# Differential attention with a post-norm feed-forward layer on one core: the attention's loops over the heads written out on every engine

## The reference, cut to what matters

```
q1, q2, k1, k2, v = x @ Wq1, x @ Wq2, x @ Wk1, x @ Wk2, x @ Wv        # split into 16 heads
a1 = softmax(causal(q1 @ k1.T / 4));  a2 = softmax(causal(q2 @ k2.T / 4))
out = (a1 - lam[h] * a2) @ v                                           # lam from lq1, lk1, lq2, lk2
merged = normalise_over_32(out) * (1 - LAM_INIT), heads side by side
x = layernorm(x + merged @ Wo)
h = silu(x @ w1.T * s1) * (x @ w2.T * s2);  h = gelu(h @ h1.T * hs1);  h = gelu(h @ h2.T * hs2)
x = layernorm(x + h @ w3.T * s3)
```

## Time and profile before

| | |
|---|---|
| three runs | 2097.49, 2097.8, 2099.39 us; median 2097.8 us |
| span of the profiled execution | 2091.4 us, 6.4 us under the median of the runs; its own time is not listed apart |
| mean granted TensorE clock | 0.961 of full speed |
| PE, ACT, DVE, POOL busy | 1925.5, 1468.2, 724.6, 201.2 us |
| first and last exponential (L811) | 232.88 us, 1311.27 us (end of the last group) |
| ACT idle just before an exponential | 106.6 us in 56 places, all ended by PE's scores (L830) |

### The profile page before, as it was taken

How to read it: one execution, slowest core, us unless ns; L and a number is a source line. 1 busy time by engine, 2 the same in 40 slices (tenths; PEclk the granted TensorE clock), 3 DMA queues, 4 the chain that set the end, 5 groups by cost and what they waited for, 6 DMA issues and landing times. The chain is left out here.

```text
span 2091.4 us, 36204 instructions
## 1 busy us (share of the span) xinstructions
PE 1925.5 (92%) x12400; PEld 1090.7 (52%) x12400; DVE 724.6 (35%) x1543; ACT 1468.2 (70%) x1876; POOL 201.2 (10%) x300
## 2 busy tenths in 40 slices
PE   7994599999899899998999999399999999999997
PEld 5883233333233233332333333278888888888886
DVE  5775021222122221221122212344554535445442
ACT  5663499989899899898998999254444435445452
POOL 0001111111111111111111111000000000000000
PEclk9997699999999999999999999699999999999998
DMA  8997805643366235642564340200101000110000
GB/s 264 361 354 200 134 6 78 83 62 55 51 82 83 36 51 81 83 56 32 79 82 57 52 57 11 81 1 31 31 11 31 22 22 21 33 31 11 11 11 12
DMA packets 137064, 148.83 MB, mean 71 GB/s; under 512 B 76000, under 2 KB 108256, under 8 KB 133760
## 3 DMA queue, kind: packets, MB, share of 16 engines
q1 hardware_dynamic: 134768, 140.55, 33.8%
q10 hardware_dynamic: 1888, 5.24, 1.3%
q0 software_dynamic: 240, 0.66, 0.2%
HBM read 90.85 MB, written 55.57 MB: 70 GB/s over the span
## 5 line engine op out<-in xcount | busy, mean ns | idle before, releaser
L811 ACT ACTIVATE attn_probs<-attn_s_ps 128x1024 f32<-128x1024 f32 (+2 forms) x1152 | 1013.5, 1049 | 112.8 <-PE attn_s_ps L830 106.6
L850 PE MATMUL attn_sums_ps<-attn_probs,heads_v 128*32 128x512 f32 (+3 forms) x5120 | 611.9, 551 | 0.0
L830 PE MATMUL attn_s_ps<-heads_q,heads_k 50*128 50x512 f32 (+3 forms) x2560 | 475.0, 435 | 93.4 <-DMA heads_q<-shift 48.5
L830 PEld LDWEIGHTS attn_s_ps<-heads_q,heads_k 50*128 50x128 f32 x2560 | 218.1, 188 | 577.3 <-ACT attn_probs L811 465.8
L1334 ACT ACTIVATE split_whole<-split_hid_ps,hs 128x512 f32<-128x512 f32 x128 | 88.3, 690 | 274.5 <-PE split_hid_ps L1248 274.3
L895 DVE COPY attn_sums_sb<-attn_sums_ps 128x512 f32<-128x512 f32 x64 | 44.3, 692 | 670.4 <-PE attn_sums_ps L850 666.8
L795 POOL TENSOR_SCALAR_AFFINE_SELECT attn_probs<-attn_probs 128x512 f32<-128x512 f32 x256 | 161.2, 639 | 955.8 <-ACT attn_probs L811 954.6
L1248 PE MATMUL split_hid_ps<-split_hid_b,h2t_r 128*128 128x512 f32 x1024 | 240.6, 392 | 0.0
L1248 PE MATMUL split_hid_ps<-split_hid_a,h1t_r 128*128 128x512 f32 x1024 | 238.1, 391 | 0.0
L1248 PEld LDWEIGHTS split_hid_ps<-split_hid_a,h1t_r 128*128 128x128 f32 x1024 | 190.0, 188 | 41.2 <-DVE split_hid_a L1476 1.4
L1248 PEld LDWEIGHTS split_hid_ps<-split_hid_b,h2t_r 128*128 128x128 f32 x1024 | 189.8, 188 | 38.0
(11 more groups left out here) (123 smaller groups left out, 1567.2 us busy)
## 6 DMA issues: line engine op xcount, KB each, us to landing
qk_parts<-proj_parts SPq DMA_DIRECT2D x64, 512.0 KB, 5.6
heads_q<-qk_parts SPq DMA_DIRECT2D x90, 256.0 KB
heads_k<-qk_parts SPq DMA_DIRECT2D x90, 256.0 KB
proj_w_rows<-in_L_ffn_h_w SPq DMA_DIRECT2D x16, 512.0 KB, 6.5
values<-proj_v SPq DMA_DIRECT2D x8, 1024.0 KB, 6.0
diffs<-attn_diff SPq DMA_DIRECT2D x32, 256.0 KB, 4.5
split_heads<-diffs SPq DMA_DIRECT2D x8, 1024.0 KB, 5.5
heads_v<-values SPq DMA_DIRECT2D x15, 512.0 KB
```

Source lines behind the costliest of these rows:

```text
L811: nc.scalar.activation(weights, side_by_side, ACT.Exp, scale=SCALE).then_inc(exp_done, 1)
L830: last = nc.tensor.matmul(s_ps[n % SLOTS][:, s, place * width:(place + 1) * width], k_sb[u][rows, b * SEQ + j * PARTS:b * SEQ + (j + 1) * ...
L850: last = nc.tensor.matmul(sums[c * D:(c + 1) * D, off:TILE], v_sb[u][:, b * KEY_BLOCKS + j, :], probs[k % PROBS][:, b, s, off:TILE], start ...
```

## The change

Every loop over the heads in the attention becomes a Python loop, which writes the code of all 16 heads one behind the other, on PE, SP, ACT, POOL and DVE. The head number is then a constant: no jump and no register operation is left there, and all waits compare with constants. The computation, the buffers, the semaphores and the order of the engines' work instructions stay as they are. Line numbers behind L763 fall by three.

```diff
-        def all_heads(eng, head):
-
-            head(0, 0, 0, True, False)
-            with eng.Fori(0, (HEADS - 2) // 2) as i:
-                head(2 * i + 1, 1, i, False, False)
-                head(2 * i + 2, 0, i + 1, False, False)
-            head(LAST, LAST % 2, LAST // 2, False, True)
+        def all_heads(head):
+
+            for h in range(HEADS):
+                head(h, h % 2, h // 2, h == 0, h == LAST)
...
-            all_heads(sp, head)
+            all_heads(head)
...
-            with pool.Fori(0, HEADS) as h:
+            for h in range(HEADS):
...
-            with act.Fori(0, HEADS) as h:
+            for h in range(HEADS):
...
-            all_heads(pe, head)
+            all_heads(head)
...
-            with dve.Fori(0, HEADS) as h:
+            for h in range(HEADS):
```

## The result

| | before | after |
|---|---|---|
| median | 2097.64 us (2093.87 to 2099.39, 4 runs) | 2058.75 us (2057.12 to 2059.86, 4 runs) |
| ratio, 95% interval | | 0.9819 [0.9805, 0.9833] |
| span of the profiled execution | 2091.4 us | 2057.0 us |
| first exponential to end of the last | 232.88 to 1311.05, 1078.2 us | 232.95 to 1273.18, 1040.2 us |
| end of the last exponential to end of the span | 780.35 us | 783.8 us |

The change is worth 38.9 us by the medians. The forecast was 2052.0, its range 2044 to 2063: the direction and the range held, the single value is 6.8 us too low. 34.4 us of the gain are in the two profiled spans: 37.9 in the attention, less 3.5 that the finish gives back.

What follows compares the result with a forecast made beforehand. ACT and PE were taken as balanced bounds at 64.34 us a head, with six heads lengthened by PE's taken jumps. Those jumps gave 45.8 us, all other terms 0: 2097.8 - 45.8 = 2052.0 us, range 2044 to 2063.

Steps and rivals of the forecast that it cites:

- Item 1: Attention: removing PE's six taken jumps gains 45.8 us, 7.6 each, by whole windows; silence alone would give 33 us.
- Item 2: Attention: removing PE's register operations is worth nothing, within 0.1 us a head.
- Item 3: Attention: removing jumps and register operations of ACT, POOL and DVE gains 0, at most 16.8 us in 16 heads.
- Item 4: Attention: loading written-out code, new for four engines, costs 0, at most 47 us for ACT's 14 packets.
- 250 instructions: Code loading: the estimate of how many PE instructions one 16 KB packet on q8 holds.
- Item 5: Attention: PE's code pages under the head loads cost 0, with up to 10 us kept in the range.
- rival B: Attention: PE's pages come late in 5 to 8 heads, giving 10 to 25 us back, 2062 to 2077; 8%.
- Item 6: Finish: PE's loop keeps two taken jumps, its place in a code page shifts; 0, bounds -3 to +7 us.
- The base: Whole kernel: the median of the runs is 6.4 us over the span, and the change leaves that alone.
- Rival A: Attention: register waits cost too, so ACT's gaps of 0.37 and 0.17 us go, 8.6 us more, 2043; 5%.

Runs made afterwards that it cites:

- e2: Changed kernel with only PE's and SP's head loops written out; ACT, POOL and DVE keep theirs with register waits: 2051.91 us, ratio 0.9789.
- e12: Kernel before with only PE's head loop written out; SP, ACT, POOL and DVE keep theirs: 2052.29 us, ratio 0.9798.
- e5: Changed kernel, but on PE and SP heads 1 to 12 stand in a loop of two rounds, one taken jump: 2060.67 us, ratio 0.9805.
- e4: Changed kernel, but PE and SP have each pair of heads in a single-round loop, registers back, no jump taken: 2056.41 us, ratio 0.982.
- e1: Changed kernel with ACT's two waits exchanged, scores first and free buffer second: 2054.89 us, ratio 0.9805.
- e3: Changed kernel with only ACT's, POOL's and DVE's loops written out; PE and SP keep theirs: 2093.64 us, ratio 1.0002 to the kernel before.
- after_again: The changed kernel run once more without any edit: 2056.87 us, ratio 0.9813.
- e6: Changed kernel with 11 unused semaphore increments on PE at the start of each head from 2 on: 2053.37 us, ratio 0.9783.
- e8: Changed kernel with SP issuing the next head's 13 loads in groups of three, waiting for each group to land: 2056.02 us, ratio 0.979.
- e9: Changed kernel with ACT's two waits exchanged and SP's head loads in groups of three: 2051.35 us, ratio 0.9777.
- e7: Changed kernel with 11 unused PE semaphore increments a head from 2 on, and 179 more before head 0: 2083.17 us, ratio 0.9916.
- e11: Changed kernel with only PE's and SP's head loops written out, SP's loads in threes, PE's finish loop also written out: 2047.54 us, ratio 0.9767.

## Why the prediction was right, and where it was off

**Item 1, PE's jumps.** Right in mechanism and in size. In e2 and e12 fifteen heads take 15 x 64.34 = 965.1 us, where before they took 431.83 + 9 x 64.34 = 1010.9: 45.8 us. Of this the branch itself is 3.3 to 3.8 us in each of six; the rest is PE's start, the lower clock and the chain filling again, and e5 shows that this rest is the part that varies. That it should be read from the whole window and not from the 5.5 us of silence was the choice that mattered: 33 us would have missed.

The Trainium skill, page "Runtime: NRT & Kernel Launch", section "Instruction fetch mechanics", says that a taken branch out of the pages held forces a fetch before execution can go on. The trace agrees: 67 ns where the branch falls through in e4, 3.3 us where it jumps, with two packets of code at the jump.

**Item 2, PE's register operations.** Right: e4 has them all and has the heads of the changed kernel.

**Item 3, jumps and register operations of ACT, POOL and DVE.** The removal is worth nothing, as taken (e2). What failed is the step that replaced them: "I take 0" covered only what goes. The order of the changed kernel showed two waits on one exponential, and the prediction priced them as code to be loaded, not as an instruction between the late signal and the work. That costs 0.27 us a head, 4.1 us, on an engine busy for 98% of the time. The term should have been added with a sign of its own; e1 takes it away by exchanging two lines.

**Item 4, new code loading.** Right: q14 has 23 packets over 942 us, a little under the 25 to 40 named, and no gap of ACT ends in anything but PE's scores. The "250 instructions" were counted loosely, from matmuls and weight loads alone and over 123 of a round's 136 us; the changed kernel's trace, 1012 recorded PE instructions in a head of 64.6 us and a packet every 16.2 us, gives 254.

**Item 5 and rival B, pages under the loads.** Mostly right. The event exists and has the form that rival B gave it, a stop of PE as head loads drain, and the prediction's own sign of it (an ACT gap over 1 us, 1.87 us in head 9) came. But it hit three heads of one execution for 3.4 us and none of another, not five to eight for 10 to 25. The 10 us kept for it in the range were enough.

**Item 6, the finish.** Taken as 0, it came out at +3.4 and +3.9 us in the two profiled executions of the changed kernel. That lies within its bounds of -3 to +7, but by luck: the bounds came from the jumps, and in the first of the two executions the tiles that hold them changed by 0.2 and 0.0 us only. The loss stands at the start of the finish, for which the item had no term. Other kernels of the study put it in a row; the time is from the first transpose of the finish to the end of the span:

| kernel | start to first feed-forward matmul | whole finish |
|---|---|---|
| before, e3 (PE looped in the attention) | 23.87, 23.88 | 753.4, 753.3 |
| after, after_again | 25.12, 23.89 | 756.8, 757.3 |
| e1, e2, e12 | 27.58, 27.58, 27.59 | 758.7, 760.9, 760.0 |
| e4, e6, e8, e9 | 25.11 or 25.12 | 756.6 to 759.0 |
| e5, e7 | 23.89, 25.12 | 754.6, 756.0 |
| e11 (its own loop written out) | 23.88 | 752.0 |

Where PE's code is as before, the finish is as before to 0.1 us, in one profile of each kernel; where it is written out, the unchanged finish is 1.2 to 7.5 us longer. The first stretch comes in three lengths only. The window of the longest, in e2, with a granted clock of 0.56, against 0.71 before:

```profile
1290.04:1317.62 27.58, 17.34 (x72) 15.14 (x72) 11.32 (x29) 4.48 (x8) 2.04 (x2) 0.56 0.13 39
```

The granted clock goes with these three lengths. PE does nothing for 23.8 to 24.1 us before the first transpose of the finish, in every trace, and starts again at the low level of the clock, 1.2 GHz (0.50). How long that level lasts from the transpose on differs; the windows end where it ends, before, after, after_again and e2:

```profile
1338.04:1344.93 6.89, 5.74 (x25) 4.94 (x25) 3.09 (x5) 1.17 (x2) 0.00 (x0) 0.50 0.00 0
...
1300.25:1311.11 10.86, 9.51 (x40) 8.31 (x40) 3.43 (x6) 1.76 (x3) 0.00 (x0) 0.50 0.00 0
...
1297.88:1303.58 5.70, 5.15 (x23) 4.75 (x24) 2.40 (x4) 0.78 (x2) 0.00 (x0) 0.50 0.00 0
...
1290.04:1308.52 18.48, 15.27 (x64) 13.57 (x64) 5.06 (x8) 2.34 (x4) 2.04 (x2) 0.50 0.20 58
```

In all fourteen traces the stretch is 23.9 us where the low level ends within 6.9 us, 25.1 where it ends after 10.6 to 11.3, and 27.6 where it lasts 18.5 us or more. The code alone doesn't decide it: after and after_again are the same program, with 10.86 and 5.70 us. Head 0, which also follows a pause of PE, does the same: 46.6 to 46.9 us where the low level ends 7.2 to 7.6 us after the first exponential, 48.8 where it ends 13.0 us after it (before), 50.1 at 15.5 us (after_again). What remains of the loss, 2.1 us in after and 3.8 us in e2, is clock in part (tile 0) and stays open otherwise.

So executions differ by up to 3.7 us at each of these two places with the clock, the work being the same. In e2 the heads gain 45.9 us and head 0 gains 2.2, and the finish loses 7.5: its span is 40.5 us shorter, not 45.9.

**The base.** "The median is 6.4 us over the span" was taken as a constant, and it is not. In the runs that list both, the device time is 1.7 to 3.0 us over the span, mostly 1.8; in the profiled execution of after 2058.76 against 2057.0. The profiled execution of before must then have taken 2093.1 to 2094.4 us, about 4 us under its median: the windows are those of a quick execution, and the forecast took them off the median of slower ones. Longer executions of before have a lower mean clock (spans of 2089.4 us at 0.962 and 2105.5 us at 0.954 in the rounds of e5), so their jumps may have cost more, as e5's did; no such execution has a trace, so this is not shown. Before's medians on other occasions were 2093.59, 2097.87, 2096.06 and 2095.31 us.

Between the two spans the sum closes: 2091.4 - 45.8 + 4.1 (waits) + 3.4 (late pages) + 0.4 (up to and in head 0) + 3.4 (finish) = 2056.9, and 2057.0 was measured. These terms are read from the two traces that they explain, so the closing is a check of completeness; that the waits and the jumps are what their terms say is shown by e1 to e4 and e12. The forecast had missed 11.3 us of losses. But the medians lie 38.9 us apart where these terms give 34.5, and the 4.4 us more hid a part of what was missed. That is luck: the losses alone would have put the time at 2063.3, just outside the range.

**The rest of the working.** Rival A's time, 2043, lies just under the range that was said to take in most of it. It didn't come: no head is shorter than 64.3 us in any run.

## What to carry to other kernels

Look for taken branches on PE in the profile's queue rows: if one takes microseconds while others on the same line take 50 ns, and packets of its code come at the jump, the code at the target has to be loaded again, and the price is read from the window around it, not from the branch. Write out only the engine that pays; the others gained nothing here, and one of them lost by it. Where an instruction has two waits, the late one belongs on the work itself: here that meant to write it first, and the trace tells which of the two became an instruction of its own.

## What the runs showed of the hardware that was not expected

- An extra semaphore instruction between a late signal and an exponential: 0.06 us each time it is really waited for, 0.27 us a head.
- 179 semaphore increments in a row on PE took 27.3 us, 0.15 us each, and are no free filler ahead of a wait of 5 us; 11 at the start of each head cost nothing (e6).
- A taken jump on PE behind which code has to be loaded costs 3.3 to 3.8 us in the branch but 6.5 to 10.7 us in the loop around it; the granted clock falls to 0.50 for 6.8 to 13.7 us there.
- Code pages of PE can arrive late as 13 head loads drain, with stops of 0.5 to 1.9 us, in some executions of a program and not in others.
- The start of an unchanged phase took 23.9, 25.1 or 27.6 us and nothing in between, by how long the clock stayed at 0.50; two executions of the same program differed by 1.2 us there.
